# Where a maximum's product stands between the two halves of a key tile's scores

## The chip, the cores and the metric

The kernel runs on one core of one Trainium2 chip. The metric is the time of one execution on the device in microseconds (us); with the kernel before and the changed one it is compared as the median of several runs. TensorE (PE), VectorE (DVE), ScalarE (ACT), GpSimd (POOL) and SyncE (SP) each work through a queue of their own, and wait for each other by semaphores.

## The reference

Eight images of 32 x 32 positions with 96 channels go through an attention with relative positions (called layer 0 here), then a causal attention (layer 1), then a mixture of four experts. Both attentions have 6 heads of 16 channels and 1024 queries and keys.

```python
# layer 0, after a group norm
attn = einsum('bqd,bkd->bqk', q * SCALE, k)
attn = attn + rel_h[:, :, :, :, None] + rel_w[:, :, :, None, :]
attn = softmax(attn, axis=-1)
x = x + einsum('bqk,bkd->bqd', attn, v) @ proj_w + proj_b
# layer 1, after a layer norm
att = where(causal, einsum('bqhd,bkhd->bhqk', q, k) * scale, min)
t = t + einsum('bhqk,bkhd->bqhd', softmax(att), v) @ w_proj
# experts, after a layer norm: top 2 of 4, gelu(x @ w1 + b1) @ w2 + b2
```

## The kernel before

The images are worked one after another. For each, `attention(it, 1)` does layer 1, `attention(it, 0)` does layer 0 of the next image, and a stage `mix` does the experts together with the products around them. A prologue prepares the first image, so that layer 0 runs eight times and layer 1 eight times.

**An attention stage** takes the six heads in three pairs (`p` = 0, 1, 2) and the keys in eight tiles of 128 (`kt` = 0 to 7). For one key tile TensorE computes, for both heads of the pair (`hh`), scores of the keys against the queries into `psT`: two products of 512 queries (`c` = 0, 1), in layer 0 at L746, in layer 1 at L749 with a mask product at L751. In layer 1 the queries in front of the key tile are left out; from key tile 4 on the half `c` = 0 has no product at all. ScalarE exponentiates each head's scores in one instruction (L1143) into `probs`. `values(p, kt - 1)` (L768 and L776) multiplies the tile before with the values, into `psO`; it stands behind the four score products of tile `kt`. So one key tile is: four score products, then four products of values (eight records in the trace).

**The maximum.** The softmax needs each query's maximum over the keys before its scores are used. It is computed a pair ahead with cheaper products: `max_scores` (L716, with a mask product L719 on layer 1's diagonal) writes 128 queries x up to 512 keys into one of the two banks of `psS`, and VectorE reduces it at once (`maxima`, L1462). I call one such product a maximum's product. Product n waits on `s_free` until the reduction of product n - 2 is done:

```python
pe.wait_ge(s_free, upto("s_free", it, st, fill - 1))
```

When all of a pair's reductions are there, VectorE joins them (L1468), TensorE transposes the row (L727, behind the values of `kt` = 6's turn), ScalarE negates it, and a DMA puts it among the operands of the next pair's scores.

**Where these products stand** is decided by `between()`. It is called at fixed points of the order on TensorE, and at its k-th call sends all of the list `ahead` up to a share of its length: `len(ahead) * k // 30`. Before, the points are behind each of the four score products of a key tile and one behind its values: five a tile, 30 in the tiles 0 to 5, by which the list is empty. The list holds 32 products in pairs 0 and 1 of layer 0 (heads of the next pair) and none in pair 2; in layer 1 it holds 18 in pair 0 (6 of the 24 are sent ahead of the loop), 32 in pair 1 (24, and 8 that are full-width products of layer 0's first pair), and 24 in pair 2 (the rest of those; none in the last image, whose pair 1 has 24). In pair 1 of layer 0, behind key tile 0, the next image's query and key products are inserted (`next_qkv`, L666), for which ScalarE must empty the `psT` slots (L1070) before the scores of tile 1's second head can go on; in pair 1 of layer 1 VectorE does the next image's group norm between the reductions (L1411 to L1444).

Of the kernel before, what the change touches and what calls it, by code (L numbers as in the profile page):

```python
# [17 lines left out]
NT = T // P  # L18
# [184 lines left out]
def upto(sem, it, stage, n):  # L203


    kind = kind_of(it)
    here = START + before(sem, stage, kind) + n
    if it is None:
        return here
    here += total(sem, "first")  # L210
    if kind == "second":
        return here
    if kind == "last":
        return here + total(sem, "second") + (B - 3) * PER[sem] + total(sem, "pre")
    return it * PER[sem] + (total(sem, "second") - PER[sem] + here)


def att_t(layer, n):

    return ("attn0b", n - QKV_AT) if layer == 0 and n >= QKV_AT else (f"attn{layer}", n)  # L220
# [12 lines left out]
def next_layer0(it):  # L233

    return kind_of(it) in ("first", "second", "body")


def next_lead(it):

    return kind_of(it) != "last"  # L240


def t_slot(stage, n):

    return n % 2
# [6 lines left out]
def q_from(layer, kt):  # L252

    return kt * P if layer else 0


def build(nc, x_tok, x_t, consts, hots, masks, w_qkv0, b_qkv0, w_p0, b_p0, rel_h, rel_w, w_qkv1, w_p1, gate_w, gate_b,
          w1, b1, w2, b2, out):
    with ExitStack() as ctx:
# [382 lines left out]
        def _(pe):  # L642
            mm = nc.tensor.matmul

            def take_t(it, stage, n):

                pe.wait_ge(t_free, upto("t_free", it, stage, n - 1))
                return psT[:, t_slot(stage, n), :]
# [81 lines left out]
            def attention(it, layer):  # L730
                st, v = f"attn{layer}", vs[layer]

                def scores(p, kt, hh, between):

                    h, q0, keys = 2 * p + hh, q_from(layer, kt), slice(kt * P, (kt + 1) * P)
                    ts, n = att_t(layer, (p * NT + kt) * 2 + hh)
                    if ts == "attn0b" and n < 2 and next_layer0(it):
                        pe.wait_ge(r_free, upto("r_free", it, "qkv0", n + 1))
                        o = psT[:, t_slot(ts, n), :]
                    else:  # L740
                        o = take_t(it, ts, n)
                    for c in range(NC):
                        a, b = max(q0, c * HALF), (c + 1) * HALF
                        if a < b:
                            if layer == 0:
                                last = mm(o[:, a:b], ks[:, p % 2, hh, keys], qs[:, p % 2, kt // 2 % 2, hh, a:b], start=True,  # L746
                                          stop=True)
                            else:
                                last = mm(o[:, a:b], kr[:, h, keys], qr[:, h, a:b], start=True, stop=a != q0)  # L749
                                if a == q0:  # L750
                                    last = mm(o[:, a:a + P], ident_b[:, :], mask_k[:, :], start=False, stop=True)  # L751
                        if c == NC - 1:
                            last.then_inc(t_full, 1)
                        between()

                def values(p, kt):

                    if kt == 0:
                        if layer == 1 and p == 0:
                            pe.wait_ge(y_free, upto("y_free", it, st, 0))  # L760
                        pe.wait_ge(o_free, upto("o_free", it, st, p))
                    for hh in range(2):
                        ts, n = att_t(layer, (p * NT + kt) * 2 + hh)
                        pe.wait_ge(t_free, upto("t_free", it, ts, n + 1))
                        for c in range(NC):
                            j = 32 * (2 * hh + c)
                            if layer == 0:
                                last = mm(psO[j:j + 2 * HD, :], v[:, kt, p, hh * HD:(hh + 2) * HD],  # L768
                                          probs[:, (2 * kt + hh) % 4, c * HALF:(c + 1) * HALF], start=kt == 0,
                                          stop=kt == NT - 1)  # L770
                                continue
                            first = (kt + NC - 1 - c) // NC
                            if first == NT // NC:
                                continue
                            every = probs[:, (2 * kt + hh) % 4, :].rearrange("p (i c q) -> p c i q", c=NC, q=P)
                            last = mm(psO[j:j + 2 * HD, first * P:HALF], v[:, kt, p, hh * HD:(hh + 2) * HD], every[:, c, first:],  # L776
                                      start=kt == 0, stop=kt == NT - NC + c)
                        last.then_inc(p_used, 1)

                n = PER_PAIR[layer]  # L780
                lead = layer == 1 and next_lead(it)
                if layer == 1:
                    pe.wait_ge(l1_in, upto("l1_in", it, "attn1", 0))
                    for fill in range(LEAD):
                        max_scores(it, st, fill)
                for p in range(PAIRS):

                    next_q = layer == 0 and p == 1 and next_layer0(it)
                    skip = LEAD if layer == 1 and p == 0 else 0
                    ahead = [(st, f) for f in range(p * n + skip, (p + 1) * n)] if p + 1 < PAIRS else []  # L790
                    if lead and p:
                        early = range(LEAD_EARLY) if p == 1 else range(LEAD_EARLY, len(MAX_STEPS["lead"]))
                        ahead += [("lead", f) for f in early]
                    points, sent = [0], [0]

                    def between():

                        points[0] += 1
                        until = min(len(ahead), len(ahead) * points[0] // (5 * (NT - 2)))
                        for stage, fill in ahead[sent[0]:until]:  # L800
                            if stage == "lead" and fill == 0:
                                pe.wait_ge(ab_in, upto("ab_in", it, "lead", 0))
                                pe.wait_ge(rel_lead_bf, upto("rel_lead_bf", it, "lead", 0))
                            max_scores(it, stage, fill)
                        sent[0] = until

                    pe.wait_ge(negmax_in, upto("negmax_in", it, st, 16 * p))
                    if layer == 0:
                        pe.wait_ge(pair_in[p % 2], upto(("pair_a_in", "pair_b_in")[p % 2], it, st, PAIR_LOADS * (p // 2 + 1)))
                    for kt in range(NT):  # L810
                        if layer == 0 and kt in (4, 6):
                            c = kt // 2 % 2
                            pe.wait_ge(turn_in[c], upto(("turn_a_in", "turn_b_in")[c], it, st, 16 * (p + 1)))
                        for hh in range(2):
                            scores(p, kt, hh, between)
                        if kt >= 1:
                            values(p, kt - 1)
                        between()
                        if kt == 0 and next_q:
                            next_qkv(it, "qkv0")  # L820
                        if kt == 0 and layer == 1 and p == 1 and next_layer0(it):
                            group_means(it, "gn")
                        if kt == NT - 2 and p + 1 < PAIRS:
                            transpose_max(it, layer, p + 1)
                        elif kt == NT - 2 and lead:
                            transpose_max(it, 0, 0)
                        if layer == 0 and p == PAIRS - 1 and it is not None:

                            if kt == 1:
                                res_norm(it)  # L830
                            elif kt == NT - 2:
                                tr_norm(it)
                    values(p, NT - 1)
# [156 lines left out]
            def next_qkv(it, st):  # L990

                pe.wait_ge(xnt_gn, upto("xnt_gn", it, "gn" if st == "qkv0" else "p_gn", 1))
                for s in range(2):
                    qk(0, take_t(it, st, s), s)
                if st == "p_qkv0":
                    for b in range(2):
                        val(0, take_t(it, st, 2 + b), b)
                    pe.wait_ge(ta_free, upto("ta_free", it, st, 2))
# [736 lines left out]
```

## Time and profile before

| | us |
|---|---|
| median of 3 runs | 2025.92 |
| lowest, highest | 2019.78, 2031.45 |
| the profiled execution | 2028.4 |
| its span in the trace | 2026.6 |
| TensorE busy | 1719.8 (85%) |
| VectorE busy | 1217.0 (60%) |
| ScalarE busy | 1071.3 (53%) |
| GpSimd busy | 297.9 (15%) |
| mean granted clock of TensorE | 0.93 |

The busy share of an engine is a mean over stages with different limits. The start of a TensorE record is when the product is taken up; its length holds the way through the array, so successive products overlap in the records. A product that had to wait shows the wait in brackets, and its weight load (PEld) waits with it. The chain of work that ended last lies on TensorE for 60% of the span, and on VectorE for 21%, of which the reduction at L1462 is 9%.

### The profile page before, as it was taken

To read this page: it belongs to the slowest core of one execution; us is meant where nothing else is said; L and a number is where in the kernel's file an instruction comes from. 1 tells how busy PE (TensorE), PEld (TensorE's weight loads), DVE (VectorE), ACT (ScalarE), POOL (GpSimd) and SP (SyncE) were. 2 spreads that over 40 slices of the span, in tenths; PEclk is the share of its full clock that TensorE was granted. 3 is DMA by queue.
4 is the path that set the end of the run, shared out by engine and by line. 5 is a ranking of instruction groups with operands and counts; after the bars stand their busy time and mean duration, and the time that the engine had idled before them with its cause. 6 is when DMAs were issued, how large, how long until landed. Compare 5 with 4: busy or idle time off the path is not lost.

```text
span 2026.6 us, 24544 instructions
## 1 busy us (share of the span) xinstructions
PE 1719.8 (85%) x8928; PEld 687.1 (34%) x8928; DVE 1217.0 (60%) x2498; ACT 1071.3 (53%) x1377; POOL 297.9 (15%) x191
## 2 busy tenths in 40 slices
PE   1578488998899988998899988999889989998858
PEld 0122232343333433344333433334333433234333
DVE  6743577546764577636775467646775466744631
ACT  1236435674556734665456745567445745565433
POOL 6103101401032000501023010321005010200000
PEclk7589679999999999999899999999999999999979
DMA  6645454445535346444335355353454454323000
GB/s 174 137 88 158 116 135 79 104 113 171 93 65 154 87 129 112 103 119 156 71 74 121 96 171 101 65 157 104 123 95 103 117 158 84 75 52 93 14 11 8
DMA packets 63742, 212.10 MB, mean 105 GB/s; under 512 B 17414, under 2 KB 19079, under 8 KB 51206
## 3 DMA queue, kind: packets, MB, share of 16 engines
q1 hardware_dynamic: 61702, 210.04, 42.0%
q8 instruction: 71, 1.16, 0.3%
q10 hardware_dynamic: 1920, 0.49, 0.1%
q14 instruction: 49, 0.40, 0.1%
HBM read 115.62 MB, written 81.79 MB: 97 GB/s over the span
## 4 chain that ended last, share of the span: by engine, by line
PE 60%; DVE 21%; ACT 7%; DMA 6%; issue 4%; SPq 2%; POOL 0%; ACTq 0%; DVEq 0%
PE psS L716 13%; DVE mx L1462 9%; PE psOM L768 9%; PE psT L746 7%; PE psT L889 5%; PE psOM L776 5%; PE psS L903 5%; PE psT L749 4%; DVE mrow L1564 3%; DVE qs L1591 2%; PE psT L666 2%; ACT probs L1143 1%; DVE x L1573 1%; DMA qs<-negr 1%; DMA qs<-scr_h 1%
## 5 line engine op out<-in xcount | busy, mean ns | idle before, releaser
L1143 ACT ACTIVATE probs<-psT 128x1024 f32<-128x1024 f32 (+7 forms) x768 | 621.4, 836 | 490.4 <-PE psT L746 240.3
L1462 DVE TENSOR_REDUCE mx<-psS 128x1 f32<-128x512 f32 (+3 forms) x1152 | 680.7, 640 | 292.2 <-PE psS L716 227.1
L746 PE MATMUL psT<-qs,ks 128*128 128x512 f32 x768 | 344.8, 522 | 38.3 <-DMA qs<-negr 17.6
L716 PE MATMUL psS<-ka,qa 128*128 128x512 bf16 x768 | 306.0, 407 | 45.2 <-DVE mx L1462 26.2
L768 PE MATMUL psOM<-probs,v 128*32 128x512 f32 x1536 | 225.5, 610 | 1.3
L716 PEld LDWEIGHTS psS<-ka,qa 128*128 128x128 bf16 x768 | 72.3, 98 | 345.4 <-DVE mx L1462 282.0
L749 PE MATMUL psT<-qr,kr 97*128 97x512 bf16 (+3 forms) x576 | 184.1, 348 | 4.6 <-DMA qr<-negb 3.7
L889 PE MATMUL psT<-xf,w1s 97*128 97x512 f32 x384 | 185.3, 616 | 1.8 <-DVE mrow L1564 1.8
L746 PEld LDWEIGHTS psT<-qs,ks 128*128 128x128 f32 x768 | 144.0, 200 | 116.7 <-ACT probs L1143 41.9
L903 PE MATMUL psS<-probs,w2s 128*96 128x512 f32 x384 | 181.5, 598 | 0.8 <-ACT att L1202 0.8
L1591 DVE TENSOR_TENSOR qs<-psOM,qs 32x768 fp32r<-32x768 f32 x128 | 121.8, 952 | 95.9 <-ACT qs L1177 93.9
L776 PE MATMUL psOM<-probs,v 128*32 128x384 f32 (+3 forms) x1440 | 148.0, 437 | 16.5 <-ACT probs L1143 16.5
L1194 ACT ACTIVATE probs<-psT 128x1024 f32<-128x1024 f32 x96 | 98.2, 1023 | 116.3 <-PE psT L889 115.7
L716 PE MATMUL psS<-kr,qr 96*128 96x512 bf16 (+3 forms) x384 | 134.5, 361 | 25.0 <-DVE mx L1462 20.5
L1564 DVE TENSOR_REDUCE mrow<-psT 128x1 f32<-128x128 f32 (+7 forms) x128 | 91.4, 753 | 52.0 <-PE psT L937 51.0
L1322 POOL TENSOR_TENSOR lb<-lb,il 96x1024 f32<-96x1024 f32 x7 | 16.6, 2369 | 711.8 <-ACT il L1167 711.8
L1276 POOL TENSOR_TENSOR split<-au,split 96x1024 bf16<-96x1024 f32 x8 | 17.0, 2126 | 600.0 <-ACT split L1094 600.0
L889 PEld LDWEIGHTS psT<-xf,w1s 97*128 97x128 f32 x384 | 71.5, 195 | 84.1 <-issue 74.7
L1573 DVE SCALAR_TENSOR_TENSOR x<-psOM,g,x 128x96 f32<-128x96 f32 x256 | 60.4, 309 | 59.6 <-PE psOM L921 59.6
L934 PE MATMUL psT<-kr,qr 96*128 96x512 bf16 (+1 forms) x192 | 54.0, 355 | 39.0 <-DVE mrow L1564 14.4
L903 PEld LDWEIGHTS psS<-probs,w2s 128*96 128x96 f32 x384 | 58.5, 164 | 82.2 <-issue 73.8
L751 PE MATMUL psT<-mask_k,ident_b 128*128 128x128 bf16 x384 | 83.2, 226 | 0.0
(165 smaller groups left out, 1711.8 us busy)
## 6 DMA issues: line engine op xcount, KB each, us to landing
qs<-scr_w SPq DMA_DIRECT2D x48, 512.0 KB, 5.3
qs<-scr_q SPq DMA_DIRECT2D x48, 384.0 KB, 7.4
scr_q<-split SPq DMA_DIRECT2D x32, 384.0 KB, 4.1
scr_k<-split SPq DMA_DIRECT2D x32, 384.0 KB, 4.6
scr_w<-qs SPq DMA_DIRECT2D x8, 1536.0 KB, 12.4
scr_h<-qs SPq DMA_DIRECT2D x16, 768.0 KB, 14.7
qs<-scr_h SPq DMA_DIRECT2D x96, 128.0 KB, 5.1
qr<-scr_q SPq DMA_DIRECT2D x8, 1152.0 KB, 7.9
```

Source lines behind the costliest of these rows:

```text
L716: last = mm(bank[:, 0:n], q[0:rows, h, t * P:(t + 1) * P], k[0:rows, h, kc * HALF:kc * HALF + n], start=True, stop=not diagonal)
L746: last = mm(o[:, a:b], ks[:, p % 2, hh, keys], qs[:, p % 2, kt // 2 % 2, hh, a:b], start=True, stop=True)
L749: last = mm(o[:, a:b], kr[:, h, keys], qr[:, h, a:b], start=True, stop=a != q0)
L768: last = mm(psO[j:j + 2 * HD, :], v[:, kt, p, hh * HD:(hh + 2) * HD], probs[:, (2 * kt + hh) % 4, c * HALF:(c + 1) * HALF], start=kt == 0, ...
L776: last = mm(psO[j:j + 2 * HD, first * P:HALF], v[:, kt, p, hh * HD:(hh + 2) * HD], every[:, c, first:], start=kt == 0, stop=kt == NT - NC + c)
L889: last = mm(o[:, c * HALF:(c + 1) * HALF], w1s[:, a:a + P], xf[:, c * HALF:(c + 1) * HALF], start=True, stop=True)
L903: last = mm(psS[0:C, c, :], w2s[:, n, :], hbuf[:, n % 4, c * HALF:(c + 1) * HALF], start=j == 0, stop=j == HJ - 1)
L1143: A(probs[:, n % 4, q0:T], psT[:, t_slot(ts, m), q0:T], ACT.Exp).then_inc(t_free, 1)
L1194: A(hbuf[:, n % 4, :], psT[:, t_slot(stage, fill), :], ACT.Gelu).then_inc(ta_free, 1)
L1462: V.reduce_max(mx[layer][:, p % 2, (h % 2) * NT + t, kc:kc + 1], psS[:, s_bank(st, fill), 0:max_cols(layer, t, kc)], AX).then_inc(s_free, 1)
L1564: V.reduce_max(mrow[:, 0, 0, n:n + 1], psT[:, t_slot(st, fill), 0:cols], AX).then_inc(t_free, 1)
L1591: ins = V.tensor_tensor(rest[0], rest[1], lead[0].bitcast(F32), ALU.subtract)
```

## The change

The point behind the first half of the first head's scores (`hh` = 0, `c` = 0) is taken out. A new point stands behind the second head's second half, just ahead of the values, next to the point that is there already; key tile 0, which has no values ahead of it, doesn't get it. Key tile 0 has four points then and the others five, 29 up to the end of tile 5, and the share is computed with 29.

```diff
                         if c == NC - 1:
                             last.then_inc(t_full, 1)
-                        between()
+                        if hh or c:
+                            between()
...
                         points[0] += 1
-                        until = min(len(ahead), len(ahead) * points[0] // (5 * (NT - 2)))
+                        until = min(len(ahead), len(ahead) * points[0] // (5 * (NT - 2) - 1))
...
                         for hh in range(2):
                             scores(p, kt, hh, between)
                         if kt >= 1:
+                            between()
                             values(p, kt - 1)
                         between()
```

All products and reductions stay as they are, and the order on VectorE, ScalarE, GpSimd and SyncE too; only the order on TensorE changes. Three places show how. In the rows, L746 and L749 are scores, L716 and L719 a maximum's product, L751 the mask of a score tile, L768 and L776 (L769 and L777 in the changed kernel) the values, L666 the next image's queries and keys.

TensorE, layer 0, pair 0: key tile 1 and the first product of tile 2, before:

```order
L746 MATMUL psT<-qs,ks 128x512
L716 MATMUL psS<-ka,qa 128x512
L746 MATMUL psT<-qs,ks 128x512
L716 MATMUL psS<-ka,qa 128x512
L746 MATMUL psT<-qs,ks 128x512
L716 MATMUL psS<-ka,qa 128x512
L746 MATMUL psT<-qs,ks 128x512
L716 MATMUL psS<-ka,qa 128x512
L768 MATMUL psOM<-probs,v 32x512 x4
L716 MATMUL psS<-ka,qa 128x512
```

The same place in the changed kernel, with the first rows of tile 2:

```order
L746 MATMUL psT<-qs,ks 128x512 x2
L716 MATMUL psS<-ka,qa 128x512
L746 MATMUL psT<-qs,ks 128x512
L716 MATMUL psS<-ka,qa 128x512
L746 MATMUL psT<-qs,ks 128x512
L716 MATMUL psS<-ka,qa 128x512 x2
L769 MATMUL psOM<-probs,v 32x512 x4
L716 MATMUL psS<-ka,qa 128x512
L746 MATMUL psT<-qs,ks 128x512 x2
L716 MATMUL psS<-ka,qa 128x512 x2
```

The product between the first two score products went to the values. With 32 products over 29 points a point sends two now and then: before these were the last points of tiles 2 and 5, now the first points of tiles 2 and 4 and the last of tile 5. Tile 0 sends four products where it sent five.

TensorE, layer 0, pair 1: key tile 0, the next image's queries and keys, and tile 1 up to its values, before:

```order
L716 MATMUL psS<-ka,qa 128x512 x2
L666 MATMUL psT<-xg,wqkv 96x512 x4
L746 MATMUL psT<-qs,ks 128x512
L716 MATMUL psS<-ka,qa 128x512
L746 MATMUL psT<-qs,ks 128x512
L716 MATMUL psS<-ka,qa 128x512
L746 MATMUL psT<-qs,ks 128x512
L716 MATMUL psS<-ka,qa 128x512
L746 MATMUL psT<-qs,ks 128x512
L716 MATMUL psS<-ka,qa 128x512
L768 MATMUL psOM<-probs,v 32x512 x4
```

And changed:

```order
L716 MATMUL psS<-ka,qa 128x512 x2
L666 MATMUL psT<-xg,wqkv 96x512 x4
L746 MATMUL psT<-qs,ks 128x512 x2
L716 MATMUL psS<-ka,qa 128x512
L746 MATMUL psT<-qs,ks 128x512
L716 MATMUL psS<-ka,qa 128x512
L746 MATMUL psT<-qs,ks 128x512
L716 MATMUL psS<-ka,qa 128x512 x2
L769 MATMUL psOM<-probs,v 32x512 x4
```

Ahead of the third score product, which is the second head's first, two maximum's products stood, and one does now.

TensorE, layer 1, pair 0: key tile 2 up to its values, before:

```order
L749 MATMUL psT<-qr,kr 128x256
L751 MATMUL psT<-mask_k,ident_b 128x128
L749 MATMUL psT<-qr,kr 128x512
L716 MATMUL psS<-kr,qr 128x128
L719 MATMUL psS<-mask_q,ident_b 128x128
L749 MATMUL psT<-qr,kr 128x256
L751 MATMUL psT<-mask_k,ident_b 128x128
L749 MATMUL psT<-qr,kr 128x512
L716 MATMUL psS<-kr,qr 128x256
L719 MATMUL psS<-mask_q,ident_b 128x128
```

And changed:

```order
L749 MATMUL psT<-qr,kr 128x512
L716 MATMUL psS<-kr,qr 128x512
L719 MATMUL psS<-mask_q,ident_b 128x128
L749 MATMUL psT<-qr,kr 128x256
L751 MATMUL psT<-mask_k,ident_b 128x128
L749 MATMUL psT<-qr,kr 128x512
L716 MATMUL psS<-kr,qr 128x128
L719 MATMUL psS<-mask_q,ident_b 128x128
L716 MATMUL psS<-kr,qr 128x256
L719 MATMUL psS<-mask_q,ident_b 128x128
L777 MATMUL psOM<-probs,v1 32x384
```

Here 18 products stood three to a key tile, one of them behind the values; now three stand in front of this tile's values, two of them next to each other, and none behind them.

## Rows read from the trace of the kernel before

**Rows 1.** The page: the span, and the reductions in its list of groups.
```profile
span 2026.6 us, 24544 instructions
...
L1462 DVE TENSOR_REDUCE mx<-psS 128x1 f32<-128x512 f32 (+3 forms) x1152 | 680.7, 640 | 292.2 <-PE psS L716 227.1
```

**Rows 2.** Waits of the whole span: who for whom, us, times, longest.
```profile
PEld psS L716 <- DVE mx L1462: 392.4, 745, 1.7
```

**Rows 3.** Timeline of TensorE, layer 0 pair 0, tile 2: start, length, instruction.
```profile
810.50 0.39 PE L716 MATMUL psS<-ka,qa 128*128 128x512 bf16 x1
...
810.96 0.39 PE L716 MATMUL psS<-ka,qa 128*128 128x512 bf16 x1
...
811.67 0.39 PE L716 MATMUL psS<-ka,qa 128*128 128x512 bf16 x1
...
812.87 0.39 PE L716 MATMUL psS<-ka,qa 128*128 128x512 bf16 x1
813.18 1.07 PE L768 MATMUL psOM<-probs,v 128*32 128x512 f32 x8
814.18 0.60 PE L716 MATMUL psS<-ka,qa 128*128 128x512 bf16 x2
```

**Rows 4.** Timeline of VectorE over the same tile and the next.
```profile
810.92 3.08 DVE L1462 TENSOR_REDUCE mx<-psS 128x1 f32<-128x512 f32 x5 [0.61 <-PE psS L716]
814.61 3.68 DVE L1462 TENSOR_REDUCE mx<-psS 128x1 f32<-128x512 f32 x6 [0.61 <-PE psS L716]
```

**Rows 5.** Timeline of TensorE, layer 0 pair 1, tile 6: nothing between scores.
```profile
858.00 1.28 PE L746 MATMUL psT<-qs,ks 128*128 128x512 f32 x4
859.22 1.06 PE L768 MATMUL psOM<-probs,v 128*32 128x512 f32 x8
```

**Rows 6.** Timeline of TensorE, layer 0 pair 1, tiles 0 and 1.
```profile
832.97 0.39 PE L716 MATMUL psS<-ka,qa 128*128 128x512 bf16 x1
...
835.35 0.39 PE L716 MATMUL psS<-ka,qa 128*128 128x512 bf16 x1 [0.21 <-DVE mx L1462]
...
840.28 0.50 PE L746 MATMUL psT<-qs,ks 128*128 128x512 f32 x1 [0.18 <-ACT kr L1070]
840.62 0.39 PE L716 MATMUL psS<-ka,qa 128*128 128x512 bf16 x1
...
841.40 1.07 PE L768 MATMUL psOM<-probs,v 128*32 128x512 f32 x8
```

**Rows 7.** Timeline of TensorE, layer 0 pair 0, tiles 0 and 1.
```profile
804.19 0.65 PE L716 MATMUL psS<-ka,qa 128*128 128x512 bf16 x1
...
805.07 0.65 PE L716 MATMUL psS<-ka,qa 128*128 128x512 bf16 x1
...
807.38 0.39 PE L716 MATMUL psS<-ka,qa 128*128 128x512 bf16 x1
...
809.50 1.07 PE L768 MATMUL psOM<-probs,v 128*32 128x512 f32 x8
```

**Rows 8.** Windows: busy us of each engine, then granted clock, DMA share, GB/s.
```profile
803.00:806.50 3.50, 3.50 (x8) 1.38 (x8) 2.07 (x3) 1.34 (x2) 0.00 (x0) 0.55 0.16 38
806.50:826.00 19.50, 18.72 (x88) 5.72 (x88) 16.61 (x27) 12.94 (x13) 9.64 (x5) 0.99 0.15 41
```

**Rows 9.** Timeline of TensorE, layer 1 pair 0, tile 5: two maximum's products.
```profile
750.57 0.39 PE L716 MATMUL psS<-kr,qr 96*128 96x512 bf16 x1
...
751.74 0.39 PE L716 MATMUL psS<-kr,qr 96*128 96x512 bf16 x1
```

**Rows 10.** Timeline of TensorE, layer 1 pair 1: tile 1's values, tile 4's last product.
```profile
761.41 1.07 PE L776 MATMUL psOM<-probs,v 128*32 128x512 f32 x8
...
773.50 0.38 PE L716 MATMUL psS<-ka,qa 128*128 128x512 bf16 x1 [1.36 <-DVE mx L1462]
```

**Rows 11.** Timeline of TensorE, layer 1 pair 2, tile 4.
```profile
793.22 0.39 PE L716 MATMUL psS<-ka,qa 128*128 128x512 bf16 x1
...
795.32 0.85 PE L776 MATMUL psOM<-probs,v 128*32 128x256 f32 x8
```

## The prediction

> **What bounds the kernel now.** I read the page first: TensorE is the busiest engine, and one kind of VectorE work, the reductions, fills 680.7 us of the span and follows TensorE closely [rows 1]. Then the whole span's waits: the weight load of a maximum's product waits on a reduction 745 times, 392.4 us in all [rows 2]. What such a wait costs only the timelines tell, so I took one image from layer 1's start (734 us) to layer 0's end (890 us), where the moved products stand.
>
> In pairs 0 and 1 of layer 0 a key tile is held by TensorE and VectorE in turn [rows 3, 4]. Call the product behind the values A, those that follow B, C, D, E. A starts at 810.50, its reduction 0.42 later (810.92). C needs A's bank and starts at 811.67, which is A + 1.17. From there the reductions follow at 0.60 each (six in 3.68 us against five in 3.08), so D comes at 1.77 and E at 2.37 (812.87). The values start 0.31 behind E and hold TensorE for 1.00, up to the next A at 3.68. VectorE meanwhile runs dry for 0.61 us a tile. The chain is thus A, its reduction, three more gates, E, values. TensorE alone would need less: four score products with nothing between take 1.22 less the 0.28 or so between A and a score, about 0.24 each [rows 5], a maximum's product 0.22, so 4 x 0.24 + 5 x 0.22 + 1.00 = 3.1 of the 3.68 us. A tile with a sixth product takes 0.60 more.
>
> **Part 1: B comes late.** In layer 0 both halves of the first head now stand between A and B. B started at A + 0.46 [rows 3], a product and a score; now a second score lies ahead of it, so it starts at 0.70 and can be reduced from 0.70 + 0.42 = 1.12. VectorE is free for it at 0.42 + 0.60 = 1.02. Before, B was there in time. Now D, E and the values shift by 0.10 us. C at 1.17 is not touched. The other scores fit: C, D and E are held at the same gates anyway, and of the score that used to separate D from E nothing is on the path, since E waits for C's reduction in either order. This holds for the tiles 2 to 5: 4 x 0.10 = 0.4 us a pair. The bounds of this term are 0 (VectorE a little slower at taking B up before as well) and 0.24, the whole score product.
>
> **Part 2: a product leaves tile 0 and comes back later.** Tile 0 has no values and sends four instead of five. The missing one is made up as an extra one in tile 4, a gated stretch, where it costs the full 0.60. What does leaving tile 0 save?
> - Pair 0: TensorE's clock is at 0.55 of full there, so about half the time at its lower level of 1.2 GHz, with 0.99 after [rows 8]. A product less is about 0.43 us less, and the gate of tile 1's B (807.38) opens earlier with it: by hand, with the same gates, tile 1's values come at 809.03 instead of 809.50 [rows 7], -0.47. Where the clock is high, the same working gives -0.28. I take -0.4, so with the 0.6 of tile 4 and the 0.4 of part 1 the pair costs +0.6, in eight images: 4.8 us.
> - Pair 1: B comes 0.24 later (it stood at 832.97), D and the last product are gated 1.17 and 1.77 behind it, so the tile ends at 834.98 instead of 835.35 [rows 6], -0.37. But then come the next image's query and key products, and a third score held at 840.28 by ScalarE's emptying of `psT`. Before it two maximum's products were sent, now one. With everything 0.37 earlier the score goes at 839.91, C at 840.25, D at 840.71 and E at C + 1.17 = 841.42, values at 841.73 instead of 841.40: +0.33. With 0.6 and 0.4 that is +1.33, in seven images; the eighth has no such insertion and costs +0.7. Together 10.0 us.
>
> Layer 0: 14.8 us. Its pair 2 has no maximum's product; it only shifts.
>
> **Part 3: layer 1.** The same gate of 1.17 for full-width products is seen at 750.57 and 751.74 [rows 9]. Most tiles of pair 0 have three maximum's products and little waiting, so TensorE's own work is the bound and each new hold counts in full. In tile 2 full-width product 11 starts, 12 follows 0.61 later behind three scores and a mask, 13 would go at 0.73 and is held until 1.17: 0.44. In tile 3 the third (now adjacent) would go 0.84 behind the first, of 384 columns, whose gate is about 1.04: 0.20. In tile 5 the gate of rows 9 stays, but one score and mask less lie under it: 0.24. Sum 0.9 us, in eight images: 7.0.
>
> Pair 1 sends mixed widths. Tile 0 and 1 together lose two held products ahead of tile 1's values, which come 0.73 earlier than 761.41 [rows 10]. In tiles 2 to 4 the lag is made up between gates, and the hold of 1.36 us at 773.50, which the group norm between the reductions makes, is met 0.4 us later relative to the values of tile 3. By hand tile 4's values stand at +0.05: nothing.
>
> Pair 2 had none at the removed point already, four products a tile. Tiles 0 and 1 win 0.32, tiles 2 and 3 read alike; tile 4 gets a fifth in front of its values (+0.60 on the 2.10 us from 793.22 to 795.32) and none behind, so tile 5 starts its chain a score and mask later, +0.27 [rows 11]. Sum +0.55. The seven images with such pairs give 7 x (0.05 + 0.55) = 4.2, and the last image's pair 1, which is of this form, 0.5.
>
> Layer 1: 11.7 us. **Sum: 14.8 + 11.7 = 26.5 us**, made against the profiled execution's 2028.4, so 2054.9 on it, and from the median of 2025.92 about **2052**. No cover swallows the shift: the stages follow each other on TensorE, and what comes late in pair 2 of layer 0 and in the expert stage (DMAs, GpSimd's splits) is set off by the attention itself.
>
> **A rule on the clock.** In the tiles with waits, 806.5 to 826 us, the granted clock is 0.99 though TensorE is held at nearly every product [rows 8]. The Trainium skill, in "TensorE: Matmul & The Clock Gate", section "A second HAM failure mode: psum-queue depth-cycling", tells of a kernel in which short idles between groups of products, from cycling through PSUM banks, made the clock fall back. The row doesn't agree for the holds as they are now; by the row the sum keeps 26.5 us, by the rule more holds would cost more, as in the second rival.
>
> **Rivals.**
> - *The lead is kept, and it gets faster.* Place: tiles 0 and 1 of each pair, whose values come up to 0.47, 0.73 and 0.32 us earlier. If the product made up later fell into VectorE's dry 0.61 us and cost nothing, and B's lateness too, the sum would be 8 x (-0.4 - 0.73 - 0.32) = -11.6 in these pairs and +0.33 x 7 in the other: about -9 us, 2017. It decides whether the extra product of a tile costs less than about 0.2 us instead of 0.60. Against it: a sixth product did cost 0.60 before [rows 4]. Chance 0.04.
> - *The clock falls.* If the longer holds bring the lower level in a quarter of the 512 products of layer 0's pairs 0 and 1, a product and the next would lie 0.88 apart as from 804.19 to 805.07 [rows 7] instead of 0.60: 128 x 0.28 = 36 us more, 2088. Chance 0.05.
> - *It hardly matters.* B is taken up in time after all (-6.4), scores that reach ScalarE 0.24 us earlier free `psT` in time for the held score of pair 1 (-5), and half of layer 1's holds don't show (-6): 9 us, 2035 or less. For it: starts worked out are good to some 0.05 us, half of part 1's delay. Against: three errors have to agree. Chance 0.16, of which 0.10 within 0.5%.
> - *As worked out*, between 2038 and 2066, chance 0.75.
>
> **How the numbers follow.** 0.5%, some 10 us, is about what a measurement of this kernel can tell from no change. Faster by more than that: 0.03 (most of the first rival, which lies at this edge). Within it: 0.13 (0.10 of the third, the rest of the first, and 0.02 of my own case for what measurements stray). Slower: 0.84 (the rest). The range reaches from 2036, the milder case, to 2066, with part 1 at its upper bound (8 x 2 x 4 x 0.14 = 9 us more) and some of layer 1's pair 1 unhidden.
>
> **What would show it.** In the changed trace, layer 0's five-product tiles from A to A at 3.78 us instead of 3.68, with VectorE dry for 0.6 and again for about 0.1 in front of B; pair 1's tile 1 values about 6 us behind the insertion's start instead of 5.8; a wait of 0.2 to 0.4 before the second of two adjacent products in layer 1's pair 0; an unchanged count of all instructions; a mean clock of 0.93. I am wrong if the tiles stay at 3.68, if ScalarE's or a DMA's waits shrink by more than a few us, or if the expert stage changes its length.

## The result, and the profile after

| | before | changed |
|---|---|---|
| median, us (5 runs each) | 2028.59 | 2045.22 |
| lowest, highest | 2019.78, 2033.05 | 2042.84, 2052.09 |
| span of the profiled execution | 2026.6 | 2046.2 |
| ratio, 95% interval | | 1.0089, [1.0062, 1.0115] |

The change makes the kernel slower by 0.9%, some 18 us by the ratio (the medians lie 16.6 apart). The forecast was slower by 26.5 us: 2052 from the median shown then, with a range from 2036 to 2066. The page of the changed kernel and its waits, which answer to [rows 1, 2]:

```profile
span 2046.2 us, 24546 instructions
...
L1464 DVE TENSOR_REDUCE mx<-psS 128x1 f32<-128x512 f32 (+3 forms) x1152 | 687.0, 642 | 307.8 <-PE psS L716 251.9
```

```profile
PEld psS L716 <- DVE mx L1464: 375.1, 712, 1.7
...
DVE mx L1464 <- PE psS L716: 251.9, 224, 13.4
...
PE psS L716 <- DVE mx L1464: 72.5, 220, 1.6
```

And the last of these rows before:

```profile
PE psS L716 <- DVE mx L1462: 46.7, 128, 1.4
```

The weight loads' waits for reductions have fallen, from 392.4 to 375.1 us, though the kernel is slower. But part of the waits of a maximum's product is booked to the product itself and not to its weight load, and that row, which [rows 2] leave out, has grown from 46.7 to 72.5 us: together 439.1 before and 447.6 now. VectorE's idle time in front of the reductions has grown from 292.2 to 307.8 us. Such a sum over the span doesn't say where the time goes; the tiles do. TensorE and VectorE in layer 0's pair 0, the image of [rows 3, 4] (start, length, instruction):

```profile
820.92 0.39 PE L716 MATMUL psS<-ka,qa 128*128 128x512 bf16 x1
820.96 0.81 PE L746 MATMUL psT<-qs,ks 128*128 128x512 f32 x2
821.61 0.39 PE L716 MATMUL psS<-ka,qa 128*128 128x512 bf16 x1
...
822.09 0.39 PE L716 MATMUL psS<-ka,qa 128*128 128x512 bf16 x1
...
822.79 0.39 PE L716 MATMUL psS<-ka,qa 128*128 128x512 bf16 x1
823.39 0.39 PE L716 MATMUL psS<-ka,qa 128*128 128x512 bf16 x1 [0.21 <-DVE mx L1464]
823.71 1.06 PE L769 MATMUL psOM<-probs,v 128*32 128x512 f32 x8
824.71 0.39 PE L716 MATMUL psS<-ka,qa 128*128 128x512 bf16 x1
```

```profile
821.34 3.18 DVE L1464 TENSOR_REDUCE mx<-psS 128x1 f32<-128x512 f32 x5 [0.61 <-PE psS L716]
825.13 3.79 DVE L1464 TENSOR_REDUCE mx<-psS 128x1 f32<-128x512 f32 x6 [0.61 <-PE psS L716]
```

A to A is 3.79 us where it was 3.68. C starts 1.17 behind A as before; B starts at 0.69 (worked out: 0.70); D comes 1.87 behind A instead of 1.77, E at 2.47, the values at 2.79. On VectorE the five reductions take 3.18 us from first to last instead of 3.08, and the dry 0.61 behind the values is unchanged: the new 0.10 lies inside the row of five, in front of B's reduction. In all eight images the five-product tiles take 3.77 to 3.80 us and the six-product ones 4.37 to 4.40.

Between fixed points of each image (the transposed maxima at L727, the inserted products at L666, the row at L984 that ends the expert stage) the two traces differ by these steps:

| stretch | forecast an image | measured, us an image | sum of measured |
|---|---|---|---|
| layer 0 pair 0 | +0.6 | -0.46, 0.70, -0.21, -0.38, -0.49, -0.50, -0.50, 1.75 | -0.1 |
| layer 0 pair 1, seven images | +1.33 | -0.36 and +1.70 in each | +9.4 |
| layer 0 pair 1, the eighth | +0.7 | 0.74 | +0.7 |
| layer 1 pair 0 | +0.9 | 0.58 to 1.62 | +8.4 |
| layer 1 pair 1 | +0.05 | -0.89 to 0.32 | -0.4 |
| layer 1 pair 2, seven images | +0.55 | 0.53 to 0.56 | +3.8 |
| expert stages and what stands between | 0 | -3.2 to 1.8 | -2.3 |

The sum is +19.6, the difference of the spans.

Two rows of the table hold steps that no gate makes. The granted clock of TensorE tells them apart. Pair 1 of layer 1 before, in the first and the second image (window, its length, busy time of PE, PEld, DVE, ACT, POOL, then the granted clock):

```profile
286.01:312.43 26.42, 22.15 (x152) 8.20 (x152) 20.67 (x48) 11.10 (x20) 0.00 (x0) 0.94 0.62 106
518.42:543.77 25.35, 20.88 (x151) 8.04 (x152) 20.64 (x48) 11.10 (x20) 0.00 (x0) 1.00 0.66 109
```

In the first six images, whose pair 1 has the same work, it took 26.42 us at 0.94 in two of them and 25.34 or 25.35 at 1.00 in the other four; in the changed kernel 25.53 to 25.55 at 1.00 in all six. So at an equal clock the change costs this pair 0.20 us an image, and the two steps near -0.9 are a stretch at the lower level (1.2 GHz) that fell away. The expert stages go the same way. Those of images 2 to 6, in all twelve traces of this document: 105.0 to 106.7 us where the granted clock was 1.00 (30 stages), 106.5 to 108.2 at 0.98 (21) and 108.4 to 109.4 at 0.97 (9).

### The profile page after: what moved, and what is told of

It reads as the page before. It is cut to its first block, busy times and chain, and to the rows that moved or that the text cites. A ratio compares the mean times of both kernels' runs of the same rounds, so it can differ in the third digit from the quotient of the medians.

```text
span 2046.2 us, 24546 instructions
## 1 busy us (share of the span) xinstructions
PE 1713.7 (84%) x8928; PEld 692.7 (34%) x8928; DVE 1223.3 (60%) x2498; ACT 1064.4 (52%) x1377; POOL 297.7 (15%) x191
## 4 chain that ended last, share of the span: by engine, by line
PE 52%; DVE 29%; ACT 7%; DMA 6%; issue 4%; SPq 2%; ACTq 0%; POOL 0%; DVEq 0%
DVE mx L1464 17%; PE psS L716 9%; PE psOM L769 9%; PE psT L891 5%; PE psOM L777 5%; PE psT L746 5%; PE psS L905 4%; PE psT L749 3%; DVE mrow L1566 3%; DVE qs L1593 2%; PE psT L666 2%; ACT probs L1145 1%; DVE x L1575 1%; DMA qs<-scr_h 1%; DMA qs<-negr 1%
## 5 line engine op out<-in xcount | busy, mean ns | idle before, releaser
L1464 DVE TENSOR_REDUCE mx<-psS 128x1 f32<-128x512 f32 (+3 forms) x1152 | 687.0, 642 | 307.8 <-PE psS L716 251.9
L716 PE MATMUL psS<-ka,qa 128*128 128x512 bf16 x768 | 302.5, 400 | 68.4 <-DVE mx L1464 46.2
L746 PE MATMUL psT<-qs,ks 128*128 128x512 f32 x768 | 303.4, 489 | 39.9 <-DMA qs<-negr 15.8
L769 PE MATMUL psOM<-probs,v 128*32 128x512 f32 x1536 | 224.0, 606 | 1.3
L716 PEld LDWEIGHTS psS<-ka,qa 128*128 128x128 bf16 x768 | 72.6, 97 | 350.3 <-DVE mx L1464 283.9
L749 PE MATMUL psT<-qr,kr 97*128 97x512 bf16 (+3 forms) x576 | 180.1, 351 | 4.6 <-DMA qr<-negb 3.7
L746 PEld LDWEIGHTS psT<-qs,ks 128*128 128x128 f32 x768 | 139.0, 196 | 118.5 <-ACT probs L1145 41.3
L777 PE MATMUL psOM<-probs,v 128*32 128x384 f32 (+3 forms) x1440 | 146.8, 434 | 16.5 <-ACT probs L1145 16.5
L716 PE MATMUL psS<-kr,qr 96*128 96x512 bf16 (+3 forms) x384 | 132.9, 359 | 30.2 <-DVE mx L1464 26.3
L751 PE MATMUL psT<-mask_k,ident_b 128*128 128x128 bf16 x384 | 83.4, 226 | 0.0
```

Source lines behind the costliest of these rows:

```text
L716: last = mm(bank[:, 0:n], q[0:rows, h, t * P:(t + 1) * P], k[0:rows, h, kc * HALF:kc * HALF + n], start=True, stop=not diagonal)
L1464: V.reduce_max(mx[layer][:, p % 2, (h % 2) * NT + t, kc:kc + 1], psS[:, s_bank(st, fill), 0:max_cols(layer, t, kc)], AX).then_inc(s_free, 1)
```

## Experiments

Theory G (gates) is the forecast's: a maximum's product waits for the reduction of the one before last, and each stretch's length follows from these gates. Its rivals are a cost of two neighbouring products by themselves, and the clock of TensorE.

**Both kernels once more**, without an edit.

> The changed kernel once more, for a second trace and a ratio beside the runs below. The first trace is 19.6 us longer in span than that of before. Theory G (gates: a maximum's product waits for the reduction of the one before last): the steps between fixed points of an image repeat, layer 0's tiles lie 3.78 to 3.79 us and 4.39 us apart, pair 1 of layer 0 +1.34 us against before in each of seven images. Theory C (clock: part of the difference is which stretches TensorE's clock is low in, and these fall by chance): the total strays by 3 to 8 us between traces of one kernel, and the low stretches at the start of layer 0's pair 0 (five of eight images before, one changed) come and go. Rival F: they are fixed by the kernel's order, and the second trace has the same ones. Ratio 1.005 to 1.013.

> The kernel before, once more, for a second trace of it. Theory C: another set of low-clock stretches than the first trace's, so layer 0's pair 0 takes a different time in some images. Rival F: low again at the start of pair 0 in the same five images. Ratio 1.00 by every theory.

Measured: the changed kernel 2050.35 us, ratio 1.0089 [1.0054, 1.0124]; before again 2026.91, ratio 0.9977 [0.9959, 0.9994], spans 2044.3 and 2028.2. The second of these intervals leaves out 1.000 although nothing was changed, so a difference of 0.2% or so means nothing here. The stretches with fixed gates repeat: pair 1 of layer 0 takes again 1.66 to 1.73 less 0.35 to 0.38 us more. The five-product tile of the image above is 3.69 in both traces of before.

The clock at the start of layer 0's pair 0 is where theory C and rival F part. The 4 us from its first score, third and fourth image (busy time of PE, PEld, DVE, ACT, POOL, then the granted clock), before:

```profile
567.30:571.30 4.00, 3.98 (x10) 1.57 (x10) 2.57 (x4) 1.97 (x2) 0.00 (x0) 0.57 0.18 41
803.00:807.00 4.00, 4.00 (x10) 1.69 (x10) 2.44 (x4) 1.84 (x2) 0.00 (x0) 0.57 0.18 41
```

The second trace of before, and then the changed kernel:

```profile
569.90:573.90 4.00, 3.69 (x14) 1.41 (x14) 3.23 (x6) 2.09 (x3) 0.00 (x0) 1.00 0.18 41
804.60:808.60 4.00, 4.00 (x10) 1.64 (x10) 2.51 (x4) 1.91 (x2) 0.00 (x0) 0.57 0.18 41
```

```profile
575.00:579.00 4.00, 3.69 (x14) 1.62 (x14) 3.00 (x5) 2.72 (x3) 0.00 (x0) 1.00 0.18 41
810.40:814.40 4.00, 3.69 (x14) 1.62 (x14) 2.99 (x5) 2.71 (x3) 0.00 (x0) 1.00 0.18 41
```

In the first image the clock is low there in every trace. Of the seven others it is low (0.57, so mostly at 1.2 GHz) in five in the first trace of before and in four in the second; in the changed kernel's traces in one and in none. So neither theory holds whole: most images repeat, one differs between the two traces of each kernel. Where the clock was high before and after, pair 0 costs 0.70, 0.68 and 0.68 us more in the changed kernel, as worked out; where it had been low, it gains 0.2 to 0.5.

**The count alone, and the place alone.**

```diff
 # count alone: tile 0 gives up its first point, the others keep theirs
-                        between()
+                        if kt or hh or c:
+                            between()
...
-                        ... points[0] // (5 * (NT - 2)))
+                        ... points[0] // (5 * (NT - 2) - 1))
```

> One part alone: in key tile 0 the point behind the first half of the scores is taken out and the share is computed with 29, as in the change; from tile 1 on all five points stay where they were before. So B (the second product of a tile) is not late, and only the product that tile 0 gives up is made up later. Theory G: layer 0's tiles back at 3.68 to 3.69 and 4.29 us, pair 1 of layer 0 +0.2 us an image, pair 0 within 0.3, layer 1 about +0.7 an image: +6 to +12 us in all, ratio 1.003 to 1.006. Rival (the count is what costs): the whole of the change's +18 us. Rival (the place is what costs): 1.000.

Measured: 2037.31 us, ratio 1.0040 [1.0019, 1.0062].

```diff
 # place alone: tile 0 keeps its points, from tile 1 on the point moves
-                        between()
+                        if not kt or hh or c:
+                            between()
...
                         if kt >= 1:
+                            between()
                             values(p, kt - 1)
```

> The other part alone: from key tile 1 on the point moves from behind the first half to the values, as in the change; tile 0 keeps its five points and the share stays at 30. Theory G: layer 0's tiles at 3.78 (five products) and 4.39 (six), pair 1 of layer 0 +1.1 us an image (0.7 behind the inserted query and key products, where one product instead of two stands ahead of the held score, and 0.1 for each of four tiles), pair 0 +0.5; in layer 1's pair 2, whose points now skip the first head's second half, B comes 0.3 later in tiles 1 to 3: about +0.9 an image. In all +15 to +24 us, ratio 1.007 to 1.012, so the parts don't add up to the change, since both hold the lag of one product. Rival (the place costs nothing): 1.000.

Measured: 2041.98 us, ratio 1.0060 [1.0039, 1.0082]. That is below the range for the total, and the reason is not in layer 0's tiles. They are as expected: with the count alone 3.68 to 3.69 and 4.28 to 4.29 us, with the place alone 3.77 to 3.79 and 4.28 to 4.29. I had written 4.39 for the last and overlooked that this kernel's extra product stands behind the values: of two products there the second keeps VectorE busy until B arrives. Pair 1 of layer 0 gave +0.23 and +1.01 us an image against 0.2 and 1.1. With the place alone I overrated layer 1's pair 2, 0.44 instead of 0.9 an image, and the low clock at pair 0's start is gone in most images here too (one of seven in each kernel), so that pair 0 gave -1.9 us in all instead of about +4. With the count alone layer 1 gave 10.3 us in all, where I had expected 0.7 an image (5.6); about 2 of it are low stretches in its pair 1 that the first trace didn't have. In the totals the count costs 0.4% and the place 0.6%; in layer 0's pair 1, where the steps repeat to some 0.03 us, the count's share is 0.23 us an image and the place's 1.01.

**One layer at a time.** The condition `hh or c`, the 29 and the new point hold for one layer only. Shown is layer 0 alone; layer 1 alone is the same the other way round.

```diff
-                        between()
+                        if layer or hh or c:
+                            between()
...
                         if kt >= 1:
+                            if not layer:
+                                between()
                             values(p, kt - 1)
```

> The change in layer 0 alone, layer 1 as before. Theory G (gates): layer 0's pair 1 +1.34 us in each of seven images, the eighth +0.7, as in the change. Pair 0 depends on the clock at its start. Theory P (the clock there is set by what stands ahead of it, layer 1 or the time at which the image comes): low again in four or five images, and pair 0 +0.5 us in them: total +10 to +14 us. Rival T (it is set by tile 0's own order): high in all, pair 0 -0.5: total +5 to +8. Layer 1's segments 0. Ratio 1.003 to 1.007.

> The change in layer 1 alone, layer 0 as before. Theory G: layer 1's pair 0 +0.8 to +1.0 us an image, pair 1 +0.2, pair 2 +0.55, about +12 us; layer 0's pair 1 exactly 0. Theory P: the clock at the start of layer 0's pair 0 is high in the four or five images where it was low, -1.0 us each, total +7 to +9. Rival T: low there as before, total +12. Ratio 1.003 to 1.006.

Measured: layer 0 alone 2043.17 us, ratio 1.0064 [1.0042, 1.0087]; layer 1 alone 2038.82, ratio 1.0046 [1.0031, 1.0061]. With layer 0 alone its pair 1 gave 1.68 to 1.72 less 0.36 to 0.38 again; with layer 1 alone its pairs gave 7.7, -0.4 and 3.8 us, and layer 0's pair 1 nothing (-0.1). For the clock these two speak for theory P. Layer 0 alone, the fifth image, and layer 1 alone, the fourth:

```profile
1043.10:1047.10 4.00, 3.96 (x10) 1.81 (x10) 2.19 (x4) 2.28 (x3) 0.00 (x0) 0.57 0.15 34
```

```profile
803.80:807.80 4.00, 3.66 (x14) 1.37 (x14) 3.19 (x6) 2.05 (x2) 0.00 (x0) 1.00 0.18 41
```

With layer 0 changed alone the clock is low at pair 0's start in four images; with layer 1 changed alone, where tile 0 of layer 0 is word for word that of before, in one. So tile 0's own order is not what decides. With the clock up, pair 0 took 0.94 to 1.23 us less in five images: that is what a low start costs here.

**Another point to the values.** This tests whether the neighbourhood costs anything by itself.

```diff
-                        between()
+                        if not kt or not hh or c:
+                            between()
...
                         if kt >= 1:
+                            between()
                             values(p, kt - 1)
```

> Another point goes to the values: from key tile 1 on the point behind the second head's first half (instead of the first head's) moves to just ahead of the values; tile 0 keeps five points and the share stays at 30. So again two maximum's products stand side by side ahead of the values, but B, the second product of a tile, stands where it stood before. Theory G: only B's lateness and the lag behind the inserted products cost anything, the neighbourhood at the values nothing: layer 0's tiles at 3.69 and 4.29 as before, pair 1 of layer 0 within 0.1 us, layer 1 within 0.5 us an image: ratio 0.998 to 1.003. Rival A (two products side by side ahead of the values cost by themselves): tiles at 3.79, ratio 1.006 or more, like the run with the place alone.

Measured: 2025.06 us, ratio 0.9989 [0.9968, 1.0010]. Its tiles take 3.68 to 3.69 and 4.28 to 4.29 us, pair 1 of layer 0 is within 0.03 an image. Rival A falls. TensorE in one of its tiles, with both products ahead of the values in the row "x2":

```profile
810.71 0.39 PE L716 MATMUL psS<-ka,qa 128*128 128x512 bf16 x1
...
811.17 0.39 PE L716 MATMUL psS<-ka,qa 128*128 128x512 bf16 x1
...
811.88 0.39 PE L716 MATMUL psS<-ka,qa 128*128 128x512 bf16 x1
...
812.56 0.90 PE L716 MATMUL psS<-ka,qa 128*128 128x512 bf16 x2
...
813.40 1.06 PE L769 MATMUL psOM<-probs,v 128*32 128x512 f32 x8
814.39 0.60 PE L716 MATMUL psS<-ka,qa 128*128 128x512 bf16 x2
```

B is back at A + 0.46 and the tile at 3.68 us. What the change costs in a tile is the point that it takes away, not the one that it adds.

**A third bank.** If the gates of two banks are the bound, one more bank should take it away. The bank is the one that otherwise holds the transposed maxima, free while pairs 0 and 1 of layer 0 send their products.

```diff
-                pe.wait_ge(s_free, upto("s_free", it, st, fill - 1))
-                bank = psS[:, s_bank(st, fill), :]
+                pe.wait_ge(s_free, upto("s_free", it, st, fill - (2 if st == "attn0" else 1)))
+                bank = max_bank(st, fill)
...
+        def max_bank(st, fill):
+            if st == "attn0":
+                return (psS[:, 0, :], psS[:, 1, :], psM)[fill % 3]
+            return psS[:, s_bank(st, fill), :]
...
-                                 psS[:, s_bank(st, fill), 0:max_cols(layer, t, kc)], AX).then_inc(s_free, 1)
+                                 max_bank(st, fill)[:, 0:max_cols(layer, t, kc)], AX).then_inc(s_free, 1)
```

> The kernel before with three PSUM banks for the maximum's products of layer 0's pairs 0 and 1 instead of two: the third is the one that otherwise holds only the transposed maxima, and a product waits for the reduction of the one three before it. Theory G (the gates of two banks hold TensorE, and VectorE runs dry behind the values because both banks are waiting when they start): a tile of five products falls from 3.68 to 3.1 to 3.3 us, VectorE's dry time behind the values from 0.61 to under 0.3, about 80 such tiles: -25 to -45 us, ratio 0.978 to 0.988. Rival (TensorE's own work or ScalarE is the bound, the waits only show who came last): within 5 us.

> The changed kernel with the same third bank. Theory G: layer 0's loss comes from the gates, so with three banks its tiles take the same time as those of before with three banks to 0.05 us; of the change's loss there remain layer 1's 10 to 13 us and in pair 1 some part of what the held score behind the inserted products costs: +8 to +16 us against the three-bank kernel before. Rival (the place ahead of the values costs TensorE time by itself, for instance in weight loads): the tiles stay 0.1 apart and the difference between the two three-bank kernels is the full 18 us.

Measured: with the order of before 1986.12 us, ratio 0.9787 [0.9764, 0.9810]; with the changed order 2002.96, ratio 0.9872 [0.9849, 0.9895]. TensorE and VectorE with three banks and the order of before:

```profile
792.13 0.39 PE L723 MATMUL psS<-ka,qa 128*128 128x512 bf16 x1
...
792.59 0.39 PE L723 MATMUL psS<-ka,qa 128*128 128x512 bf16 x1
...
793.05 0.39 PE L723 MATMUL psOM<-ka,qa 128*128 128x512 bf16 x1
...
793.51 0.39 PE L723 MATMUL psS<-ka,qa 128*128 128x512 bf16 x1
...
793.97 0.39 PE L723 MATMUL psS<-ka,qa 128*128 128x512 bf16 x1
794.29 1.07 PE L775 MATMUL psOM<-probs,v 128*32 128x512 f32 x8
795.29 0.39 PE L723 MATMUL psOM<-ka,qa 128*128 128x512 bf16 x1
```

```profile
792.55 1.29 DVE L1469 TENSOR_REDUCE mx<-psS 128x1 f32<-128x512 f32 x2
793.76 0.68 DVE L1469 TENSOR_REDUCE mx<-psOM 128x1 f32<-128x512 f32 x1
794.36 1.28 DVE L1469 TENSOR_REDUCE mx<-psS 128x1 f32<-128x512 f32 x2
795.72 0.69 DVE L1469 TENSOR_REDUCE mx<-psOM 128x1 f32<-128x512 f32 x1
```

No product is held, they follow at 0.46 us (a product and a score), and the tile takes 3.16 us, TensorE's own work. The 0.61 us in which VectorE ran dry has shrunk to about 0.1. This is 43 us for one more bank. It isn't all that the bank could give: in pair 0's tile 6 the transposing product now waits 1.22 us for VectorE's joined maxima, and that tile takes 3.74 us instead of 2.45 in seven of the eight images. The Trainium skill, in "Perfetto Trace Analysis", section "Optimizing Tensor Performance", asks that independent products rotate through different banks so that the emptying of one overlaps the next; two banks did rotate here, and the trace shows that two don't reach over a block of other products that is 1.0 us long.

With the changed order the tiles take 3.18 to 3.20 and 3.77 to 3.80 us against 3.16 and 3.68 with the order of before, so the five-product tiles agree to 0.04 and the six-product tiles don't, by 0.1. VectorE in a six-product tile of the changed order shows why:

```profile
797.07 0.69 DVE L1471 TENSOR_REDUCE mx<-psOM 128x1 f32<-128x512 f32 x1
797.77 1.29 DVE L1471 TENSOR_REDUCE mx<-psS 128x1 f32<-128x512 f32 x2
```

B's reduction follows A's at 0.70 instead of 0.60, the same lateness as with two banks. Six reductions at 0.60 are 3.6 us, so this tile is VectorE's, and the 0.10 lengthens it; a five-product tile has room for it. Layer 0 as a whole now costs nothing more (pair 0 -5.1 us in all, of which about 2 are two low starts that are gone, pair 1 +4.9), layer 1 its 9.2. But the spans differ by 16.9, more than I gave and near the rival's 18. It is not by the rival's mechanism: +8.0 us lie in the expert stages (+6.3) and behind the last transposed maxima (+1.7), without a maximum's product in them, and the granted clock is lower there. The third image's expert stage with the order of before and with the changed order:

```profile
609.64:715.59 105.95, 94.83 (x458) 43.36 (x454) 56.83 (x137) 65.50 (x79) 8.09 (x7) 1.00 0.47 140
611.09:720.09 109.00, 97.97 (x458) 44.39 (x454) 56.83 (x137) 65.42 (x79) 8.10 (x7) 0.97 0.46 133
```

Of the seven stages behind the first, two are below 1.00 with the order of before and four with the changed one; the end behind the last transposed maxima has 0.83 and 0.81. Between the first two kernels here the same stretches differed by -2.3.

**The third bank in layer 1's pair 2 too.**

```diff
+        def three(st, fill):
+            return st == "attn0" or st == "lead" and fill >= LEAD_EARLY
```

The wait and `max_bank` ask `three(st, fill)` where they asked `st == "attn0"`.

> The three-bank kernel with the order of before, and the third bank also used by the full-width products in layer 1's pair 2. Theory G: pair 2's tiles of four products, 3.10 us where the values take 1.0, are held by the same two-bank gates; TensorE's own work in them is 2.8 us, so 0.2 to 0.3 a tile, five tiles, seven images: 5 to 9 us below the three-bank kernel (whose median was 1986): 1977 to 1982, ratio 0.974 to 0.979. Rival (these tiles are at TensorE's own work already): 1986, ratio 0.979.

Measured: 1975.92 us, ratio 0.9759 [0.9720, 0.9798], below the first three-bank kernel by 10 us in the medians and 8.4 in the spans. Pair 2 of layer 1 gave 2.21 to 2.22 us an image, 15.5 in all, more than my 5 to 9; about half was given back in stretches that the edit doesn't touch: the expert stages (+6.3, with the clock below 1.00 in three of the seven behind the first instead of two, and lower in them) and pair 0 of layer 0 (+4.7), whose first score now waits up to 1.6 us for the DMA that brings the negated maxima where it waited 0.7. This is the fastest version, some 50 us under before and 69 under the changed kernel.

## Why the prediction was right, and where it was off

- *What bounds the kernel*: right. The gates, read from two tiles, gave the changed tile to 0.01 us, and the third bank shows that they are the bound. The 392.4 us of [rows 2] were only the weight loads' part of the waits.
- *Part 1, B comes late by 0.10*: right, 3.79 against 3.78 forecast. The place alone shows it without the count, and the late point moved shows its cause. "The other scores fit" was right too.
- *Part 2, pair 1*: +1.33 forecast, 1.34 measured in seven images, with the same parts: -0.37 and then 1.70. The held third score is there:

```profile
846.16 0.39 PE L716 MATMUL psS<-ka,qa 128*128 128x512 bf16 x1
846.97 0.50 PE L746 MATMUL psT<-qs,ks 128*128 128x512 f32 x1 [0.41 <-ACT kr L1072]
847.31 0.39 PE L716 MATMUL psS<-ka,qa 128*128 128x512 bf16 x1
...
848.49 0.39 PE L716 MATMUL psS<-ka,qa 128*128 128x512 bf16 x1 [0.33 <-DVE mx L1464]
848.80 1.06 PE L769 MATMUL psOM<-probs,v 128*32 128x512 f32 x8
```

  TensorE now waits 0.41 us for ScalarE where it was 0.18 [rows 6], and E is held 1.18 behind C. The values stand 6.54 us behind the insertion's start instead of 5.83. The sign was written as "about 6", though the prediction's own starts give 6.5.
- *Part 2, pair 0*: this is the term that failed, +4.8 us forecast, -0.1 measured. I took the low clock of [rows 8] as a property of tile 0 that stays. It fell away in most images when the order ahead of it in layer 1 changed. The images with a high clock before and after gave the +0.7 that the gates give, and with layer 0 changed alone three images that were low in both traces gave 0.55, 0.56 and 0.83 against the 0.6 of the sum. So the gates were right and the clock was not. The first image, low in every trace, strayed by 1.0 between the two traces of before and tells nothing.
- *Part 3*: pair 0 0.9 forecast, 1.05 measured on average; in tile 2 the third product is held as said:

```profile
750.02 0.38 PE L716 MATMUL psS<-kr,qr 96*128 96x512 bf16 x1
...
750.69 0.22 PE L716 MATMUL psS<-kr,qr 96*128 96x128 bf16 x1
...
751.25 0.28 PE L716 MATMUL psS<-kr,qr 96*128 96x256 bf16 x1 [0.28 <-DVE mx L1464]
```

  Pair 1 was put at +0.05 an image and gave -0.05 on average, which is luck: +0.20 to 0.32 in six images, and -0.9 in the two in which a low stretch fell away. Pair 2 was put at 0.55 and gave 0.55. Layer 1's sum is 11.8 against 11.7, and that close only because these errors cancel.
- *The sum*: 26.5 forecast, 19.6 between the spans. Of the 6.9 missing, 4.9 are pair 0 of layer 0 and 2.3 the expert stages. At an equal clock the change would cost more than was forecast. An estimate from the table and from the images that had it: 0.7 x 8 for layer 0's pair 0, 10.1 for its pair 1, and 8.4, 0.2 x 6 + 0.6 and 3.8 for layer 1's pairs, 29.7 us in all. By this estimate my steps for the gates were some 3 us too small together, and the low stretches that went away took more than that back. So the mechanism was right, and a part of the closeness of the total is luck.
- *A sign of being wrong* was a change in the expert stages' length. It came, -3.2 to +1.8 us an image, and goes with the granted clock and not with the moved products. I had put these stages at nothing, and had no term for how they stray.
- *The rule on the clock* would have made more holds slower. The granted clock rose instead, from 0.93 to 0.936. The second rival falls; the third was wrong in its reasons (no gate opened early) and right only in that the total came out lower than forecast.
- *What stays open*: what brings a low stretch to one image's expert stage or pair and not to another's, and which piece of layer 1's order moves those in the pairs. They are worth a few us, more than the terms that I worked out to 0.1 us.

## What to carry to other kernels

Where a small product feeds a reduction through a few banks, write down the distances of one period: product to reduction, reduction to the next product let in, and the longest block of other work between two products. Moving a product is free as long as each still arrives before its reducer is free, and costs the lateness in every period from where it doesn't; the place that it goes to matters less than the gap that it leaves. If the reducer runs dry behind the same block in each period, look for one more bank before moving anything: here it gave 43 us, where the moves cost between nothing and 18. And write the granted clock beside each duration that goes into the sum: one that was read at the lower level need not be there in the changed kernel.

## What was not expected of the hardware

A stretch at the lower clock can come and go at one place with what stands ahead of it. At the start of layer 0's pair 0 (granted clock 0.57 instead of 1.00 over 4 us) it costs about 1.1 us, and in layer 1's pair 1 1.08 us. Of the seven images behind the first it was there in 5, 4, 4, 2 and 3 in the five traces of kernels in which layer 1's pair 2, just ahead, takes the time it took before, and in 1, 0, 1, 1, 1, 0 and 1 in the seven traces in which that pair is 0.44 to 0.56 us longer or 2.2 shorter. In layer 1's pair 1, of the first six images of each trace, it was there in 12 of 30 with layer 1's order as before and in none of 24 with its order changed as in the change. These are counts from twelve traces; what in the pair's length would do it was not tested.
